# Building the routing-weight rows of an expert ahead of its gate loop instead of between the loop's first four passes

## The reference

```python
xn = layernorm(x)                                   # [4096, 1024]
# recurrent part
B_x = xn @ B_w.T + B_b
h_t = sigmoid(log_A) * h_{t-1} + B_x_t              # scan over time
s   = h @ C_w.T + C_b
# mixture of 8 experts, all computed densely, two weights per token not zero
logits = xn @ Wr + br
w, idx = top_k(logits, 2);  w = softmax(w)
c = sum(one_hot(idx, 8) * w[..., None], axis=-2)    # [4096, 8]
y_e = (silu(xn @ W1[e]) * (xn @ W3[e])) @ W2[e]     # 1024 -> 2048 -> 1024
out = x + s * silu(sum_e c[:, e] * y_e)
```

## Time and profile before

| | before |
|---|---|
| median of 3 runs | 5973.92 us (5967.87 to 6556.4) |
| the profiled execution | 5970.89 us |
| its span, slowest core (core 4) | 5969.2 us |
| spans of the 8 cores | 5951.6 to 5969.2 us |
| mean granted TensorE clock | 0.993 |
| busy in the span | PE 96%, DVE 28%, ACT 12%, POOL 11% |
| DMA | 461.72 MB, mean 77 GB/s |

### The profile page before, as it was taken

One profiled execution on the slowest core, in us unless ns is written; L12 is line 12 of the kernel. 1 busy time (PEld: TensorE's weight loads), 2 busy tenths in 40 slices (PEclk: granted clock), 3 DMA queues, 4 the chain that ended last, 5 costly groups with the idle time before them and its releaser, 6 DMA issues.

```text
span 5969.2 us, 67144 instructions; the slowest of 8 cores (5951.6 to 5969.2 us)
## 1 busy us (share of the span) xinstructions
PE 5734.1 (96%) x26384; PEld 2589.4 (43%) x26912; DVE 1682.1 (28%) x2600; ACT 714.6 (12%) x1247; POOL 679.7 (11%) x1293
## 2 busy tenths in 40 slices
PE   5999999999899999999989999999999999999998
PEld 2444444444344444444444444444444444444443
DVE  2222222223322222222332222222242122222224
ACT  2011111110110111111011101111101000101110
POOL 1111111110011111111001111111101111111110
PEclk9999999999999999999999999999999999999999
DMA  5445445443344454544344444444435444445442
GB/s 103 75 78 81 80 73 85 73 74 62 90 78 75 78 83 74 92 66 74 55 97 78 75 78 80 81 85 76 68 62 101 67 75 75 76 76 80 74 71 67
DMA packets 199410, 461.72 MB, mean 77 GB/s; under 512 B 22592, under 2 KB 22720, under 8 KB 198848
## 3 DMA queue, kind: packets, MB, share of 16 engines
q0 software_dynamic: 184848, 406.95, 42.8%
q1 hardware_dynamic: 14256, 50.44, 2.5%
HBM read 847.39 MB, written 16.78 MB: 145 GB/s over the span
## 4 chain that ended last, share of the span: by engine, by line
PE 90%; DMA 4%; issue 2%; ACT 2%; DVE 2%; DVEq 0%; SPq 0%; ACTq 0%; POOLq 0%
PE pb L343 28%; PE pb L363 28%; PE pb L470 23%; PE pb L447 3%; DMA w2s<-w 2%; PE pb L513 2%; PE pb L559 2%; PE pb L312 1%; ACT xn_all L168 1%; DMA out_s<-x 1%; DVE stats L157 1%; DMA x_p<-x 1%; ACT L380 1%; PE pb L288 0%; PE pb L459 0%
## 5 line engine op out<-in xcount | busy, mean ns | idle before, releaser
L343 PE MATMUL pb<-xnT,w1s 128*128 128x512 bf16 x8016 | 1845.7, 380 | 52.7 <-ACT silu_s L381 40.8
L363 PE MATMUL pb<-xnT,w3s 128*128 128x512 bf16 x8028 | 1841.0, 379 | 8.6
L470 PE MATMUL pb<-h_s,w2s 128*128 128x512 bf16 x7028 | 1550.7, 379 | 28.1 <-DMA w2s<-w 20.4
L343 PEld LDWEIGHTS pb<-xnT,w1s 128*128 128x128 bf16 x8192 | 796.7, 98 | 1039.6 <-issue 112.7
L363 PEld LDWEIGHTS pb<-xnT,w3s 128*128 128x128 bf16 x8192 | 801.7, 98 | 966.4
L394 DVE TENSOR_TENSOR h_s<-silu_s,pb 128x512 bf16<-128x512 f32 x512 | 351.7, 687 | 2803.7 <-PE pb L363 2770.5
L470 PEld LDWEIGHTS pb<-h_s,w2s 128*128 128x128 bf16 x7168 | 699.3, 98 | 874.4 <-issue 40.7
L380 ACT ACTIVATE silu_s<-pb 128x512 f32<-128x512 f32 x512 | 305.7, 597 | 4440.3 <-PE pb L343 4439.9
L493 DVE TENSOR_TENSOR silu_s<-pb,cbc 128x512 f32<-128x512 f32 x448 | 309.7, 691 | 905.7 <-PE pb L470 789.6
L122 POOL DMA_DIRECT2D w1s<-w x512 | 270.6, 529 | 2326.0 <-PE pb L343 2304.6
L122 POOL DMA_DIRECT2D w3s<-w x512 | 270.9, 529 | 1385.9 <-PE pb L363 1193.3
(11 more groups left out here) (64 smaller groups left out, 897.6 us busy)
## 6 DMA issues: line engine op xcount, KB each, us to landing
w1s<-w POOLq DMA_DIRECT2D x512, 256.0 KB, 4.0
w3s<-w POOLq DMA_DIRECT2D x512, 256.0 KB, 4.1
w2s<-w POOLq DMA_DIRECT2D x256, 512.0 KB, 5.7
x_p<-x SPq DMA_DIRECT2D x32, 512.0 KB, 3.8
out_s<-x SPq DMA_DIRECT2D x32, 512.0 KB, 5.6
out<-out_s SPq DMA_DIRECT2D x32, 512.0 KB, 3.0
wbw<-bwT POOLq DMA_DIRECT2D x1, 2048.0 KB, 19.0
wcw<-cwT POOLq DMA_DIRECT2D x1, 2048.0 KB, 32.1
```

The lines of the kernel that those rows point to most:

```text
L343: ins = e.matmul(pb[tc][:, :], w1s[:, bb_, k, :], xnT[:, k, tc * TC:(tc + 1) * TC], start=(k == 0), stop=(k == NK - 1))
L363: ins = e.matmul(pb[2 + tc][:, :], w3s[:, bb_, k, :], xnT[:, k, tc * TC:(tc + 1) * TC], start=(k == 0), stop=(k == NK - 1))
L470: ins = e.matmul(p[:, :], w2s[:, bb_, kk, :], h_s[:, kk, t * TC:(t + 1) * TC], start=(kk == 0), stop=(kk == NIT - 1))
```

## The change

The list `c_jobs` and the calls from inside the loop are gone. All four helpers are called one after the other at the head of the expert, before the first gate matmul of pass 0 is written out. The helpers, their waits and everything else are as they were. In the lists of the engines: on TensorE the order becomes L288, L312, L288, L312 and then the gate of pass 0; on VectorE it becomes L299, L320, L299, L320 behind the last L497 of the expert before and ahead of the `h` product of pass 0. No DMA is issued by the helpers and none changes its place.

```diff
-            c_jobs = [(emit_ctp, 0), (emit_cbc, 0), (emit_ctp, 1),
-                      (emit_cbc, 1)]
+            for fn_c, tc_c in [(emit_ctp, 0), (emit_cbc, 0), (emit_ctp, 1),
+                               (emit_cbc, 1)]:
+                fn_c(tc_c)
 
             for it in range(NIT):
                 b = it % 2
@@
                 vh = emit("vector", h_fn,
                           [("s_act", vs), ("s_pe", vu)], "s_dve")
                 ev["h", e_i, it] = vh
-                if it < len(c_jobs):
-                    fn_c, tc_c = c_jobs[it]
-                    fn_c(tc_c)
                 if it == 4 and g + 1 < ngrp:
                     emit_stats((g + 1) * 8 + e_i)
```

## The result

The changed kernel is slower by 3.5%: the ratio of its time to that of the kernel before is 1.0347, 95% interval 1.0333 to 1.0361, which is 207 us on 5973. Its runs that count took 6175.22 to 6182.03 us. The forecast was 6095 (+2.0%), in a range of 6076 to 6145. The direction was right, the size was not. (In many runs some cores spent a time at a granted clock of 0.81, whatever the kernel; the runs that this lengthened much are left out of all comparisons, single stretches of about 161 us remain in some of the others, and the text names them where they matter.)

What follows compares the result with a forecast made beforehand. TensorE, busy in 96% of the span, was taken to bound the kernel. Chain 84, group starts 28 and clock 13 us sum to 125 us on 5970.9, 6096 us; forecast 6095 us (+2.0%), range 6076 to 6145.

Steps and rivals of the forecast that it cites:

- the chain at experts 1 to 7: At 28 expert starts the four helpers run one behind the other and TensorE waits: 3.0 us each, 84 us.
- the clock at these 28: At the starts of experts 1 to 7, TensorE's clock falls at a third: 9 falls of 1.4 us, 13 us.
- the first expert of a group: At 4 starts L288 also waits for the routing chain, no longer covered by the gate: 7 us each, 28 us.
- What bounds the kernel: TensorE, busy in 96% of the span; new waits at an expert's start lengthen the run by the same amount.
- Rival (c): Pass 5: earlier normalisation removes TensorE's waits for the Silu, giving back up to 40.8 us; 6030 to 6055 us, chance 0.03.
- The queue of L299 behind the last output tile: At experts 1 to 7, L299 queues on VectorE behind L493 and L497, starting at 1.67 us and ending at 2.34.
- the third I had assumed: Share of the 28 starts of experts 1 to 7 at which the clock falls: 9 falls, 13 us.
- the one spell behind the 3.0 us wait: Clock fall in the earlier trace after a wait for `w2s`: 3.4 us at half clock, up to 1.7 us of work.
- rival (b): Expert starts: the clock falls at nearly every expert, 39 to 48 us instead of 13; 6122 to 6147 us, chance 0.25.
- The transposes' rule: L288 at the expert's head: transposes don't count as clock activity like matmuls; if so, the sum of a fall at every expert.
- my end for all at half clock: First expert of a group, whole new stretch at half clock: about 11 us each, upper end 44 us for four.

Runs made afterwards that it cites:

- the bf16 filling: Changed kernel plus 8 and 4 bf16 matmuls of 128 rows, results unread, in the two pauses of each expert's helper chain: 6088.28 us.

## Why the prediction was off, point by point

| term of the sum | predicted | measured |
|---|---|---|
| the chain at experts 1 to 7, 28 | 84 us | 82 us (6.12 - 3.19 each, with the clock held by the bf16 filling) |
| the clock at these 28 | 13 us: 9 falls of 1.4 | 85 us: 28 falls of 3.0 |
| the first expert of a group, 4 | 28 us | 38 us (37 and 39 in the runs with these alone) |
| sum | 125 us | 205 us of 207 |

*What bounds the kernel, and that nothing absorbs the new waits*: right. The waits for the Silu stayed at 24 and 40.7 us. Rival (c), which had them vanish, was wrong for the reason given.

*The chain at experts 1 to 7*: right, to 0.02 us at each step, and the filled kernel shows it without the clock. The queue of L299 behind the last output tile is real (1.89 to 0.83 us when it is taken away). I had 90 us for the 64 waits of L312 and 5 us for each of L288; they were 85.1 and 5.2.

*The clock*: here the prediction failed, in two factors. The first is how often. I compared the new stretch with the one at the group's end by the share of time in which TensorE is busy. That one consists of transposes L602 that use all 128 rows; the new one of L312 with a single row. The busy share is the same for both, and the clock does not go by it. With 128 rows in L312 the falls were 4 to 9 of 28, up to the third I had assumed: the assumption treated one-row matmuls as full work. I did write that no row shows whether such work holds the clock, and then gave it 0.25, too little for a question that no row answered in favour of my case.

The second factor is the price. I took 3.4 us at half clock from the one spell behind the 3.0 us wait, and 1.4 us of loss. A spell here was 6.9 us long and fell on the second L312 (6.99 instead of 6.12 to the gate) and the gate (5.60 instead of 3.45), 3.0 us of loss in all. Rows for a longer one were at hand: the up of the fourth group started 6.22 us behind the last logits matmul where 3.5 would do. Even with 28 falls, rival (b) was therefore too cheap, 6122 to 6147 where it measured 6178.

*The transposes' rule*: the page of the Trainium skill that I named, "TensorE: Matmul & The Clock Gate" (Part 4: PE-mode transpose), led to the right rival, a fall at every expert. But the runs show another reason for most of the falls: with L288 unchanged and only L312 at 128 rows, most of them went. Whether L288, with one column, holds the clock was not measured by itself, so the runs neither confirm nor refute the rule for it.

*The first expert of a group*: the waits were as forecast (20.7 us in 4, 5.2 each). From L288 to the gate it took 7.83 us, close to my end for all at half clock (5.37 less the 0.15 ahead of L288, and twice 0.44 + 0.9, makes 7.90), and the gate 5.36, between its ends. I had taken a value nearer the full clock. This too was the clock and not the chain.

## What to carry to other kernels

The handovers of a helper chain that bounces between two engines cost nothing while a few us of independent matmuls lie between its steps; pulled together, each handover shows in full, here 2.9 us an expert, and it can be added up beforehand from the timeline to within 0.1 us. Such a stretch has a second price that no list of waits shows: here, where little of the array was at work for a few us, TensorE's clock fell, and the next full-rate matmuls paid, as much again. So when you judge whether a stretch keeps the clock, look at the rows (the form 1*128 or 128*128) of its matmuls, and not only at TensorE's busy share.

## What the runs showed of the hardware

- Twelve one-row matmuls of 512 columns, with TensorE busy for 7.04 of 7.10 us, did not keep the clock at 1.00 (28 falls of 28). Twelve with 128 rows, in the same places, did (0 of 28).
- Rows that hold only zeros count: L312 over 128 rows, 127 of them zero, cut the falls from 28 of 28 to between 4 and 9 and took no more time (two records of 1.10 us in all instead of 1.09; 6.05 us from the first L288 to the gate at most of the starts without a fall).
- Shorter pauses alone did not hold the clock: with the first pause at 0.83 us instead of 1.89 it still fell at 27 or 28 of 28 starts, and with both pauses filled by one-row matmuls at 28.
- A column of a tile, repeated 128 times as stationary operand, with the identity as moving one, transposes and broadcasts in one fp32 matmul of about 0.22 us for 128 values, and needs no copy in between.
